# The feed-forward stage taken up inside the tile steps of a fused Mamba-and-FFN block, through one PSUM bank

## What is computed

```
def _L0_ffn_ref(x, W_r, W_k, W_v, mu_r, mu_k):
    x_prev = concat([0, x[:, :-1]])
    xr = mu_r * x + (1 - mu_r) * x_prev
    xk = mu_k * x + (1 - mu_k) * x_prev
    r = sigmoid(xr @ W_r)
    k = xk @ W_k
    return r * (square(relu(k)) @ W_v)

x = x + _layernorm(_L0_attn_ref(_layernorm(x), ...))   # the mixer
x = x + _layernorm(_L0_ffn_ref(_layernorm(x), ...))
```

## Time and profile before

| | us |
|---|---|
| median of 3 runs | 272.7 (271.68 to 273.03) |
| the profiled execution, its own time | 273.49 |
| its span in the trace | 271.7 |
| TensorE busy | 229.7 (85%) |
| VectorE busy | 196.6 (72%) |
| ScalarE busy | 194.1 (71%) |
| GpSimd busy | 168.1 (62%) |

### The profile page before, as it was taken

One profiled execution on the slowest core, in us unless ns is written; L12 is line 12 of the kernel. 1 busy time (PEld: TensorE's weight loads), 2 busy tenths in 40 slices (PEclk: granted clock), 3 DMA queues, 4 the chain that ended last, 5 costly groups with the idle time before them and its releaser, 6 DMA issues.

```text
span 271.7 us, 7118 instructions
## 1 busy us (share of the span) xinstructions
PE 229.7 (85%) x1958; PEld 176.3 (65%) x1958; DVE 196.6 (72%) x593; ACT 194.1 (71%) x727; POOL 168.1 (62%) x281
## 2 busy tenths in 40 slices
PE   0995997789899999999999999999873798989930
PEld 0993343578678788787887878877652485657730
DVE  1699999967677676776767757679565758887761
ACT  2367387689787877878778788788554386979941
POOL 6423407586686867777687786877596476774120
PEclk9999599999999999999999999999999599999995
DMA  5960000000000000000000000000000000311122
GB/s 131 224 219 2 0 0 1 0 4 2 2 2 0 2 2 0 2 0 2 2 0 0 2 2 0 2 0 4 2 0 6 5 2 1 77 36 43 41 58 58
DMA packets 10159, 6.39 MB, mean 24 GB/s; under 512 B 832, under 2 KB 9824, under 8 KB 10128
## 3 DMA queue, kind: packets, MB, share of 16 engines
q1 hardware_dynamic: 9984, 5.77, 8.5%
q0 software_dynamic: 144, 0.21, 0.4%
HBM read 3.88 MB, written 2.10 MB: 22 GB/s over the span
## 4 chain that ended last, share of the span: by engine, by line
PE 45%; DVE 19%; issue 14%; ACT 10%; POOL 7%; DMA 2%; ACTq 1%; DVEq 1%; POOLq 1%
PE bank L886 10%; PE bank L790 6%; PE bank L967 6%; PE bank L874 6%; PE bank L880 5%; ACT bt L627 3%; DVE f L1388 3%; POOL frs L508 3%; ACT bank L616 2%; DVE ff L1400 2%; PE bank L757 2%; DVE fst L1404 2%; DMA w_sb<-w_in 2%; PE bank L749 1%; POOL rb L400 1%
## 5 line engine op out<-in xcount | busy, mean ns | idle before, releaser
L1209 DVE TENSOR_TENSOR x<-bank,wx 128x512 f32<-128x512 f32 x32 | 22.1, 690 | 35.5 <-ACT bank L616 31.3
L886 PE MATMUL bank<-x,sg 64*64 64x256 f32 x256 | 34.6, 385 | 0.0
L886 PE MATMUL bank<-xg,sg 64*64 64x256 f32 x256 | 33.9, 376 | 0.0
L874 PE MATMUL bank<-x,turned_bc 64*64 64x256 f32 x224 | 29.6, 376 | 0.0
L439 POOL TENSOR_TENSOR y<-ysum,zs 128x256 f32<-128x256 f32 x32 | 23.7, 740 | 7.7 <-DVE ysum L1231 7.2
L397 POOL TENSOR_TENSOR mse<-msb,eps_all 128x2 f32<-128x2 f32 x32 | 6.9, 217 | 33.1 <-ACT junk L607 33.1
L880 PE MATMUL bank<-st,bt 64*64 64x256 f32 x128 | 20.8, 395 | 5.0 <-ACT bt L627 4.9
L886 PEld LDWEIGHTS bank<-xg,sg 64*64 64x64 f32 x256 | 21.5, 133 | 4.7
L400 POOL TENSOR_TENSOR rb<-mse,halfn 128x2 f32<-128x2 f32 x32 | 23.0, 717 | 2.5
L616 ACT ACTIVATE bank<-bank,rsn 128x512 f32<-128x512 f32 x32 | 21.2, 661 | 4.3 <-PE bank L790 1.4
L967 PE MATMUL bank<-wo_sb,yt 128*128 128x128 f32 x128 | 22.8, 301 | 0.5 <-ACT yt L633 0.5
(11 more groups left out here) (201 smaller groups left out, 771.9 us busy)
## 6 DMA issues: line engine op xcount, KB each, us to landing
x_all<-x SPq DMA_DIRECT2D x16, 128.0 KB, 3.8
out<-o_all SPq DMA_DIRECT2D x16, 128.0 KB, 2.4
cm<-consts SPq DMA_DIRECT2D x1, 640.0 KB, 6.5
w_sb<-w_in SPq DMA_DIRECT2D x1, 480.0 KB, 4.4
cm<-consts POOLq DMA_DIRECT2D x1, 128.0 KB, 3.9
wo_sb<-w_out SPq DMA_DIRECT2D x1, 128.0 KB, 4.8
bcb_sb<-bc_bias SPq DMA_DIRECT2D x1, 96.0 KB, 4.7
wr_sb<-w_r SPq DMA_DIRECT2D x1, 64.0 KB, 4.6
```

Source lines behind the costliest of these rows:

```text
L874: mm = nc.tensor.matmul(bank[5][half(1 - h), 0:DI], turned_bc[half(h), q, 2 * r], rx(x, r)[half(h)], start=(r == 0), stop=(r == R - 1))
L886: mm = nc.tensor.matmul(bank[7][half(h), 0:DI], sg[half(h), a, r], rx(x, r)[half(h)], start=start, stop=stop)
L1209: vec.tensor_tensor((x1, xg)[a][:, par].rearrange("p (a e) -> p a e", e=P), bank[1][:].rearrange("p (a e) -> p a e", e=P), wx[:, par, a].u ...
```

## The change

The last stage loses its loop. Its parts become `ffn(n)` on each engine, called at the end of the tile step n on TensorE, GpSimd and ScalarE and in the middle of it on VectorE (behind the mask, ahead of the weighting of x), and then alone for n = 33 to 47. With c, q = divmod(n, 4):

| q | VectorE | GpSimd | ScalarE | TensorE |
|---|---|---|---|---|
| 0 | norm bias of chunk c-2; `f2` of c-4 | | tanh of c-3; normed x of c-2 | v of c-3 |
| 1 | `ff` and its statistics of c-3 | carry of c-2 | outputs of c-4 | transposes of c-2 |
| 2 | factor terms of c-1; moments of c-3 | pow for c-1's factors; pow for c-3 | copies curT, prevT of c-2 | k of c-2 |
| 3 | residual, statistics and moments of c-1 | pow for c-1's layer norm | relu and square of c-2 | r of c-2 |

The first residual is VectorE's for all chunks. The factors are raised for each chunk. The tile loops of VectorE, GpSimd and ScalarE are written out. PSUM: y goes to bank 6, transposed y shares bank 3 with the scores, the output product shares bank 5 with the new state sum, and bank 7 alone serves t, k, r and v of the last stage in turn (from chunk 6 on, they have banks 7, 0, 1, 2). The sharing brings waits: `y_out(n-1)` now waits for sp of tile n, `y_turn` for the mask of n, the scores for the copy of y.

```
+        t_ps, inter_ps = bank[2][:, 0:DI], bank[2][:, DI:]
+        yt_ps, scores = bank[3][:, 0:DI], pair[:, :, DI:DI + L]
+        p_ps, o_ps, fk_ps = bank[5][:, 0:DI], bank[5][:, DI:DI + D], bank[5][:, DI + D:DI + D + H]
+        y_ps, ffn_ps = bank[6][:, 0:DI], bank[7]
+        def ffn_bank(name, c):
+            return bank[{"t": 7, "k": 0, "r": 1, "v": 2}[name]] if c >= NC_ - 2 else ffn_ps
...
             def y_turn(i, par):
                 pe.wait_ge(S["y_ready"], i + 1)
-                pe.wait_ge(S["o_sb"], i)
+                pe.wait_ge(S["sg_ready"], min(i + 2, NT))
...
+            def y_out(i, general):
                 pe.wait_ge(S["yt_sb"], i + 1)
+                    pe.wait_ge(S["p_added"], min(i + 2, NT - NQ))
+                pe.wait_ge(S["o_sb"], i)
...
+            def factors(c):                                    # GpSimd
+                pool.wait_ge(fac_v, FAC_STEPS * (c + 1))
+                nc.gpsimd.tensor_tensor(tokc[:, 7, tiles_in(c)], tokc[:, 6, tiles_in(c)], halfn[:, 0:NQ],
                                         ALU.pow).then_inc(fac_p, 1)
...
-                nc.gpsimd.tensor_tensor(o_all[:, rows], o_all[:, rows],
-                                        tokc[:, 7, rows].unsqueeze(2).broadcast_to([128, NQ, D]), ALU.mult)\
-                nc.gpsimd.tensor_tensor(x_all[:, rows], o_all[:, rows], x_all[:, rows], ALU.add).then_inc(C["x1"], 1)
...
+            def residual(c):                                   # VectorE
+                dve.wait_ge(fac_p, c + 1)
                 for q in range(NQ):
+                    i = c * NQ + q
+                    vec.scalar_tensor_tensor(out=x_all[:, i], in0=o_all[:, i], scalar=tokc[:, 7, i:i + 1],
+                                             in1=x_all[:, i], op0=ALU.mult, op1=ALU.add).then_inc(C["x1"], 1)
...
+            def norm_bias(c):
+                dve.wait_ge(C["pow"], c + 1)
...
                 if within(n):
                     mask(n)
+                ffn(n)
                 if within(n + 1):
                     weighted_x(n + 1, (q + 1) % 2, 0)
```

More of the change, by code:

```diff
@@ L50 @@
 MOM = 6
-FAC_POW = 3
+FAC_STEPS = 3
+FFN_STEPS = NT + 4 * NQ
 FLAG_AT = 6
@@ L290, in build, with valid, tiles_in @@
         fac_v, fac_p = sem("factors_vector"), sem("factors_pool")
[L292 to L309 removed]
+        def valid(c):
+            return 0 <= c < NC_
+        def tiles_in(c):
+            return slice(c * NQ, c * NQ + NQ)
         def moments(dve, stats, mo, n, chain, base, eps):
@@ new lines, in k_square, with outputs @@
+            def k_square(c):
+                act.wait_ge(C["k_relu"], c + 1)
+                wait_past(act, C["v_ps"], c)
+                nc.scalar.activation(ka[:], kr[:], ACT.Square).then_inc(C["k_act"], 1)
+            def outputs(c):
+                act.wait_ge(C["norm_bias3"], c + 1)
+                for q in range(NQ):
+                    act.wait_ge(C["res"], c * NQ + q + 1)
+                    nc.scalar.activation(o_all[:, c * NQ + q], f2[:, q], ACT.Identity,
+                                         bias=fnb[:, NQ + q:NQ + q + 1]).then_inc(C["outv"], 1)
@@ L674, in _, with ffn @@
+            def ffn(n):
+                c, q = divmod(n, NQ)
+                if q == 0 and valid(c - 2):
+                    normed(c - 2)
+                if q == 1 and valid(c - 4):
+                    outputs(c - 4)
+                if q == 3 and valid(c - 2):
+                    k_square(c - 2)
             act.wait_ge(S["st_zero"], 2)
-            for n in range(-2, NQ):
+            for n in range(-2, FFN_STEPS):
                 step(n, n % NQ)
+                ffn(n)
                 if n < 0:
@@ L737, in _ @@
-            chunks(act, chunk)
         @block.tensor
@@ L966, in y_out, with turn_normed @@
                 for k in range(2):
-                    mm = nc.tensor.matmul(bank[6][:, DI:DI + D], yt[:, k], wo_sb[:, k], start=(k == 0), stop=(k == 1))
+                    mm = nc.tensor.matmul(o_ps, yt[:, k], wo_sb[:, k], start=(k == 0), stop=(k == 1))
                 mm.then_inc(S["o_ps"], 1)
+            cur = curT[:].rearrange("p b l -> p (b l)")
+            prev = prevT[:].rearrange("p b l -> p (b l)")
+            def turn_normed(c):
+                pe.wait_ge(C["normed"], c * NQ + NQ)
+                if c == 0:
+                    pe.wait_ge(S["weights"], 4)
+                else:
+                    pe.wait_ge(C["f"], c * NQ)
+                for q in range(NQ):
+                    mm = nc.tensor.transpose(ffn_bank("t", c)[:, q * 128:q * 128 + 128], xn2[:, q], c_("ident"))
+                mm.then_inc(C["tr_ps"], 1)
@@ new lines, in project_v @@
+            def project_v(c):
+                v_ps = ffn_bank("v", c)
+                pe.wait_ge(C["k_act"], c + 1)
+                if v_ps is ffn_ps:
+                    pe.wait_ge(C["th"], c + 1)
+                else:
+                    pe.wait_ge(C["f"], c * NQ)
+                for q in range(NQ):
+                    mm = nc.tensor.matmul(v_ps[:, q * D:q * D + D], ka[:, q * 128:q * 128 + 128], wv_half[:],
+                                          start=True, stop=True)
+                mm.then_inc(C["v_ps"], 1)
@@ new lines, in ffn @@
+            def ffn(n):
+                c, q = divmod(n, NQ)
+                if q == 0 and valid(c - 2):
+                    norm_bias(c - 2)
+                if q == 0 and valid(c - 4):
+                    last_residual(c - 4)
+                if q == 1 and valid(c - 3):
+                    gated_v(c - 3)
+                if q == 2 and valid(c - 1):
+                    factor_terms(c - 1)
+                if q == 2 and valid(c - 3):
+                    moments3(c - 3)
+                if q == 3 and valid(c - 1):
+                    residual(c - 1)
+                    stats2(c - 1)
+                    moments2(c - 1)
@@ L1354, in tiles @@
                 dve.wait_ge(s2, TABLES_AT)
-                with dve.Fori(1, NC_ - 1) as c:
-                    for q in range(NQ):
-                        step(c * NQ + q, q, general)
-                for n in range(NT - NQ, NT + 1):
+                for n in range(NQ, NT + 1):
                     step(n, n % NQ, general)
```

460 lines of the change are left out of this document (195 added, 265 removed).

## The result

The changed kernel takes 299.61 us (median of 4 runs, 297.93 to 300.08), the kernel before, on the same chip, 272.63 us (271.68 to 273.03): a ratio of 1.098, with a 95% interval of 1.093 to 1.104. The forecast was 299, slower, with a range of 283 to 315. The profiled execution has a span of 298.3 us against 271.7, and a mean granted clock of 0.94.

What follows compares the result with a forecast made beforehand. TensorE bounds the tile stage; no tile work fills the last stage's 64 us. Tile stage growing from 208 to some 265 and last stage shrinking to about 33 give span 298.0, forecast 299, range 283 to 315.

Steps and rivals of the forecast that it cites:

- The two waits: VectorE idles some 3 us per chunk before the residual (q = 3) and before the norm bias (q = 0), awaiting GpSimd's powers.
- A full chunk: Four tile steps with last-stage work take 30.0 us, against 19.4 before, set by VectorE's list; TensorE needs 24.4.
- The ring: Sp, output product, last-stage piece F, projection, x and next sp follow in a loop through y_out's new wait: 5.00 + F.
- Empty steps: Tile steps without last-stage work take 5.0 us in place of 4.85.
- s+0.94 for v: At q = 1, TensorE starts v behind the output product, 0.94 us after s, the start of VectorE's sp.
- The clock: Rival: TensorE's idle gaps at q = 3 lower its clock, losing 2 to 3 us each; 316 at all seven; chance 0.12.
- a granted clock below 1.0: Sign against the prediction: the granted clock leaving 1.0 in the middle of the tile stage.
- The end: After the tile stage: ysum of tile 31 at 264.4, last chunks' chains, f2, then 6.3 us, giving a span of 298.0.
- by the bounds: Range 286 to 311 for the slower case, from bounds on first steps, factor terms, jump, end, clock falls and ScalarE; chance 0.77.
- No charge for the power beside the residual: GpSimd's power of c-3 adds nothing to VectorE's residual; by the skill's rule five residuals would come 1.0 later, 5 us.
- TensorE stays the bound: Rival: with GpSimd's results ready and VectorE's waits gone, TensorE sets the steps, 29 us less: 270; chance 0.07.
- 5.0 + F: That rival's step time: 5.0 us plus TensorE's last-stage piece F, 1.0, 0.5, 1.7, 1.8 for q = 0 to 3.

Runs made afterwards that it cites:

- e1: Changed kernel with all of GpSimd's last-stage work (powers and carry) moved ahead of the next root and y in its step: 276.23 us.
- e5: Changed kernel with only GpSimd's power for the factors moved ahead of the gated product, other powers and carry left late: 284.66 us.
- e6: Changed kernel with the output product issued one step later, behind the projection of x, and emptied by ScalarE behind its silu: 288.30 us.
- e4: Changed kernel with three unused matmuls added in TensorE's idle time, in the q = 3 steps of chunks 2 to 7: 300.02 us.
- e10: e9 with ScalarE's normed x of the last chunk moved ahead of relu, square and tanh of chunk 6: 260.77 us.
- e9: e7 with the last chunk's transposes freed from chunk 6's gated values, and VectorE's residual multiply-adds moved ahead of sp: 261.46 us.
- e7: Changed kernel with the moves of e1 and e6 together: 265.96 us.

## Why the prediction was right

Its own steps against the trace:

- **The two waits.** 3.04 us at q = 3 by the sum; 3.14 and 3.0 measured. The sum from the earlier trace rows carried it: GpSimd's list, not the power, has the price. e1 and e5 show it (23.4 us in all, 15.0 and 8.4 apart, with the clock's part in them).
- **A full chunk.** 9.4 + 8.3 + 6.1 + 6.2 = 30.0 forecast; 9.36 + 7.87 + 6.09 + 5.76 = 29.08 measured at full clock, 29.8 with a low stretch in it. The q = 0 step was 0.4 too long in the sum: norm bias to x took 1.46 (184.92 to 186.38) rather than 0.4 + 1.14 + 0.3. So was q = 2: the factor terms took 0.9 rather than 1.6, the moments beside GpSimd's work 1.6 rather than 1.2.
- **The ring.** Empty steps of 5.0: 5.01 to 5.03 measured for tiles 4 to 6; sp of tile 5 at 79.90, forecast 79.6. But I spoke of the ring for the empty steps alone and not for the steps with q = 1, where e6 shows 1.2 us of it through v. The sum came out right there because it had the wait inside: s+0.94 for v is sp, hand-over and product (0.42 + 0.05 + 0.47).
- **The clock.** I gave it 0.12 as a rival of 316 and 5 us in the range, and named a granted clock below 1.0 among the signs that the prediction would be wrong. That sign came: it did fall, at five of the seven places (the three shown, and 0.69 and 0.78 in the stretches from 209 to 213 and from 239 to 243), and cost 3.0 us at three of these places (e4), not 14 to 20 over all: a low stretch was about half as long as that of the earlier trace rows, and most of it lay under VectorE's next wait of 3 us, which was there anyway. Only the step to tile 12, which has no f2 and less cover, paid 1.5; those to tiles 16 and 24 paid 0.6 each.
- **The end.** ysum of tile 31 at 264.34 (forecast 264.4), which is luck: the steps to tile 16 took 79.7 us rather than 77.8, most of it the clock at tile 12, and the full chunks behind them less than their 30.0. Then ff of chunk 5 at 270.06 (271.6: the jump out of the branch cost 2.20 idle us on VectorE, not 3.4), ff of 6 at 280.59 (281.2: 10.5 behind that of 5 rather than 9.6, with the granted clock at 0.50 from 272 to 278, which the sum had nowhere), of 7 at 288.87 (287.7: the last chain took 8.3 rather than 6.5, since its normed x stood behind relu and tanh of chunk 6 on ScalarE; without that, e10, it takes 6.75), last f2 at 292.71 (291.7), and from there to the end 5.6 rather than 6.3. These are errors of 0.7 to 1.8 us of both signs, so the 299 is closer than its terms deserve. (The range of 286 to 311 "by the bounds" is also narrower than the bounds listed: added up they give 285 to 315.)
- **No charge for the power beside the residual.** In the rows of GpSimd and VectorE above, the power of 1.00 at 175.63 runs beside the residual at 175.69, which takes its 1.14. By the rule that the prediction weighed (the Trainium skill, GPSIMD Engine Reference, section Specifications) it would have been 1.0 longer; this row, like the 0.17 of the earlier trace rows, speaks against the rule for a power. For GpSimd's full-width products e9 bears the rule out. The Trainium skill, SBUF — State Buffer, section Summary: rules for kernel authors, has the second of the two to issue fully blocked until the first finishes. The 0.71 us that each of the four operations takes, one beside each product of 0.45 to 0.74, agrees with that.

The rival *TensorE stays the bound* was put at 270 if GpSimd's results lay ready. e1 makes them ready and gives 276.2. The rival's 5.0 + F holds for a full chunk, 25.0 against 25.4 measured (the step with q = 2 took 5.8 rather than 5.5, from VectorE's factor terms and moments). It misses in steps 6 to 16, 68.6 against 64: the step to tile 7 took 7.41 rather than 5.0, since VectorE's own list sets it, with the residual at 2.40 beside GpSimd's work (1.75 in the later chunks). Only with the ring open too (e7) is TensorE the bound, at 266.

So two things made the change slow: the place of GpSimd's small powers in its list (23.4 us) and the output product, with its new wait, ahead of v and the projection (11.3). Both numbers hold some 2 to 3 us of the fallen clock, which either move mostly takes away. Folding the work in is no loss by itself: in e9 sp of tile 27 comes 21.7 us later than in the kernel before (205.85 against 184.19), and what follows it takes 54.4 us instead of 87.5.
